# First attention of a megakernel: spikes added in PSUM, 128 tokens ahead of the rest, two powers on ScalarE, three currents on VectorE

## The reference

```python
# L0, first half: spiking mixer on h = layernorm(x)*(1+ca)+sa
r, ek, v = sigmoid(h@Wr+br), exp(h@Wk+bk), h@Wv+bv
# scan over time: wkv from running sums, inp = r*wkv
mem = 0.3*mem + inp - (mem > 0.05)*0.05
x = x + ga * (mem > 0.05)            # the spikes
# L0, second half: two layers (l = 0, 1) of local attention and MLP on
h = layernorm(x)*(1+cb) + sb
h2 = shift_token(h)                  # upper 64 channels one token later
q, k, v = split(h2 @ wqkv[l])        # 8 heads of 64
q, k = rotary(l2norm(q)*qs), rotary(l2norm(k)*ksc)
h = h + local_attention(q, k, v, window=64) @ wo[l]
h = h + gated_mlp(layernorm(shift_token(h)))
x = x + gb * h
# L1: linear recurrence, then experts (8, the best two) on x
```

## Time and profile before

| | us |
|---|---|
| median of 3 timed runs | 548.56 (548.49 to 548.58) |
| profiled execution, device time | 549.87 |
| its span | 548.1 |
| TensorE busy | 494.0 (90%) |
| VectorE busy | 427.0 (78%) |
| ScalarE busy | 349.6 (64%) |
| GpSimd busy | 339.3 (62%) |

### The profile page before, as it was taken

The page is one execution under the profiler, slowest core; times in us unless marked ns, Lnnn a source line. Parts: engine busy times, 40 slices in busy tenths (PEclk is TensorE's granted clock), DMA queues, the critical chain, the costliest instruction groups (busy, mean ns, idle before and its releaser), DMA issues.

```text
span 548.1 us, 11812 instructions
## 1 busy us (share of the span) xinstructions
PE 494.0 (90%) x4059; PEld 315.8 (58%) x4059; DVE 427.0 (78%) x1173; ACT 349.6 (64%) x1001; POOL 339.3 (62%) x271
## 2 busy tenths in 40 slices
PE   5844088999999999999899999999999999999996
PEld 5424033567777776443467777777544445667775
DVE  6999999899888976566889988995545687566665
ACT  5854007699999987534679999998556526533332
POOL 5990028999999998668989999994111277410000
PEclk9975579999999999999989999999999999999999
DMA  8600003211111112000221111111000000000000
GB/s 300 238 1 1 0 3 109 56 39 32 40 40 41 41 39 71 0 2 0 77 49 35 37 41 39 41 40 31 1 1 0 0 1 1 1 1 19 22 20 19
DMA packets 15025, 20.98 MB, mean 38 GB/s; under 512 B 2379, under 2 KB 9013, under 8 KB 14709
## 3 DMA queue, kind: packets, MB, share of 16 engines
q1 hardware_dynamic: 14676, 20.13, 13.3%
q10 hardware_dynamic: 288, 0.08, 0.1%
HBM read 9.99 MB, written 1.05 MB: 20 GB/s over the span
## 4 chain that ended last, share of the span: by engine, by line
PE 68%; DVE 18%; POOL 6%; issue 4%; ACT 3%; DMA 1%; DVEq 0%; SPq 0%; POOLq 0%; ACTq 0%
PE psT L1523 11%; PE psQK L1615 9%; PE psO L1738 6%; PE psO L1670 5%; PE psQK L1945 5%; PE psS L1718 5%; DVE vst L1108 3%; DVE vAB L1112 3%; PE psO L1523 3%; PE psS L2017 3%; PE psQK L1752 3%; PE psO L2017 2%; PE psQK L1877 2%; PE psS L1854 2%; PE psQK L1756 2%
## 5 line engine op out<-in xcount | busy, mean ns | idle before, releaser
L576 ACT ACTIVATE prob<-psS,nmx 128x128 f32<-128x128 f32 x256 | 90.1, 378 | 18.2 <-DVE nmx L1248 18.2
L904 POOL TENSOR_TENSOR rn<-ssq,half 128x16 f32<-128x16 f32 x32 | 93.2, 2913 | 8.6 <-DVE ssq L1234 8.5
L896 POOL TENSOR_TENSOR ra<-ra,rb 128x512 f32<-128x512 f32 x64 | 81.0, 1286 | 1.0 <-DVE rb L1216 0.8
L716 POOL TENSOR_TENSOR rst<-mv,half 128x4 f32<-128x4 f32 x24 | 25.7, 1072 | 73.8 <-DVE mv L1009 64.2
L1615 PE MATMUL psQK<-wqkv,hsA 128*128 128x512 f32 x128 | 62.0, 604 | 1.0 <-DVE hsA L1197 0.6
L576 ACT ACTIVATION_READ_ACCUMULATOR prob<-psS,nmx 128x1 f32 x256 | 55.4, 216 | 0.0
L912 POOL TENSOR_TENSOR qkn<-ra,rn 128x512 f32<-128x512 f32 x32 | 49.0, 1532 | 2.5
L1213 DVE TENSOR_TENSOR ra<-psQK,rope 128x512 f32<-128x512 f32 x64 | 43.9, 686 | 7.5 <-PE psQK L1615 6.6
L1216 DVE TENSOR_TENSOR rb<-psQK,rope 128x512 f32<-128x512 f32 x64 | 43.5, 680 | 0.0
L697 ACT ACTIVATE gel<-psQK 128x512 f32<-128x512 f32 x32 | 19.1, 597 | 37.5 <-PE psQK L1945 37.5
L1227 DVE TENSOR_REDUCE ssq<-sq 128x8 f32<-128x512 f32 x64 | 41.1, 676 | 1.6 <-ACT sq L516 1.3
(11 more groups left out here) (263 smaller groups left out, 1177.6 us busy)
## 6 DMA issues: line engine op xcount, KB each, us to landing
vAB<-vAB SPq DMA_DIRECT2D x62, 128.0 KB, 2.2
wqkv<-in_wqkv SPq DMA_DIRECT2D x2, 768.0 KB, 8.2
big<-in_x SPq DMA_DIRECT2D x4, 256.0 KB, 5.3
ra<-in_rope_t SPq DMA_DIRECT2D x1, 1024.0 KB, 7.7
ropeb<-in_rope SPq DMA_DIRECT2D x1, 1024.0 KB, 8.6
big<-in_ew SPq DMA_DIRECT2D x2, 512.0 KB, 4.1
wmod<-in_wmod SPq DMA_DIRECT2D x2, 384.0 KB, 6.8
out<-big SPq DMA_DIRECT2D x3, 256.0 KB, 2.3
```

The costliest lines, as they stand in the source:

```text
L576: act.activation(prob[:, k, :], psS[:, hb, c * P:(c + 1) * P], ACT.Exp, bias=nmx[:, k:k + 1], accum_out=sums[:, n % 2, k:k + 1]).then_inc( ...
L896: pool.tensor_tensor(o, o, rb[:, r], ALU.add).then_inc(s["sum_" + name], 1)
L904: pool.tensor_tensor(rn[:, :], ssq[:, :], half[:, :], ALU.pow).then_inc(s["rn_ready"], 1)
```

## The change

Seven things, all around the first tiles of layer 0:

1. VectorE takes current 1 too, from the PSUM bank, before quotient 3; GpSimd keeps current 2 only.
2. The thresholds write to a row of their own, `spikes` (big[:, 6, :]). x_cm is transposed into the four statistics banks while the membrane passes run, and TensorE then adds the spikes to each bank with ordinary products by the identity (`stack_t1`, start=False). All four thresholds come before the first statistics. x_cm itself gets the spikes at the end of layer 0, all groups on GpSimd.
3. The expert weights, whose place `spikes` has taken, are loaded in layer 1, after that layer's weights.
4. `first_norm`: ScalarE takes the first power as exp(-0.5 ln x), GpSimd only multiplies. ScalarE normalises two blocks, scales the first 128 tokens from a bank of their own into z, and then does the rest.
5. VectorE copies only these 128 tokens to hsA; the remaining 384 of group 0 go by two transfers, which the products of tiles 1 to 3 wait for.
6. `norms(0)`, the power for tile 0, is ScalarE's too, ahead of the fourth group's normalisation. The activation table that holds both functions is loaded in the place of the old load.
7. The order on all engines follows: statistics of groups 2 and 3 between tile 0's rotary products on VectorE, tile 1's products between the later transposes on TensorE.

The core of the diff:

```diff
+                    sp.wait_ge(s["ln_out"], ln_no(1, 0) + 1)
+                    sp.dma_start(hsA[0:64, P:GW], z[0:64, P:GW]).then_inc(s["hsA_dma0"], 16)
+                    sp.dma_start(hsA[64:128, P + 1:GW + 1], z[64:128, P:GW]).then_inc(s["hsA_dma0"], 16)
+                else:
                     sp.wait_ge(s["x_mixed"], NG)
...
                 act.wait_ge(s["num_ready"], min(g + 2, NG))
-                act.activation(rsg[:, gsl(g)] if g in (1, 2) else r_bank(g), r_bank(g), ACT.Sigmoid, bias=vec[:, V_BR:V_BR + 1]).then_inc(s["r_ready"], 1)
+                act.activation(rsg[:, gsl(g)] if g == 2 else r_bank(g), r_bank(g), ACT.Sigmoid, bias=vec[:, V_BR:V_BR + 1]).then_inc(s["r_ready"], 1)
...
             act.wait_ge(s["table"], 1)
+            act.preload_act_table_set("natural_log_exp_and_others")
             load_table(ACT.Exp)
...
-            ln_norm(ln_no(1, 0))
-            stack_out(0)
+            def power(dst, src):
+
+                own.one(act.activation(dst, src, ACT.Ln, bias=0.0, scale=1.0))
+                return act.activation(dst, dst, ACT.Exp, bias=0.0, scale=-0.5)
+
+            def first_norm():
+
+                n = ln_no(1, 0)
+                act.wait_ge(s["ln_var"], n + 1)
+                power(rst[:, n % 4, :], mv[:, n % 4, :, 1]).then_inc(s["rst_act"], 1)
+                act.wait_ge(s["rst_act"], 1)
+                act.wait_ge(s["ln_rstd"], n + 1)
+                act.wait_ge(s["ln_t2"], n - 1)
+                for k in range(TPG):
+                    act.activation(lnx[:, n % 2, k, :], stat_bank(n)[:, k, :], ACT.Identity, bias=nmr[:, n % 4, k:k + 1],
+                                   scale=rst[:, n % 4, k:k + 1]).then_inc(s["ln_norm"], 1)
+                    if k == 1:
+                        act.wait_ge(s["first_t2"], 1)
+                        act.activation(z[:, 0:P], psQK[:, 0, 0:P], ACT.Identity, bias=mod[:, 0, SB, 0:1],
+                                       scale=mod[:, 0, CB, 0:1]).then_inc(s["first_out"], 1)
+                act.wait_ge(s["ln_t2"], n + 1)
+                act.activation(z[:, P:GW], out_bank(n)[:, P:GW], ACT.Identity, bias=mod[:, 0, SB, 0:1],
+                               scale=mod[:, 0, CB, 0:1]).then_inc(s["ln_out"], 1)
+
+            def norms(n):
+
+                act.wait_ge(s["ssq_max"], n + 1)
+                if n:
+                    act.wait_ge(s["k_ready"], n)
+                    act.wait_ge(s["q_ready"], n)
+                power(rn[:, :], ssq[:, :]).then_inc(s["rn_ready"], 1)
+
+            first_norm()
             ln_norm(ln_no(1, 1))
+            squares_k(0)
             ln_norm(ln_no(1, 2))
             stack_out(1)
-            squares_k(0)
             squares_q(0)
+            norms(0)
             ln_norm(ln_no(1, 3))
...
                 elif n == 0:
-                    act.wait_ge(s["x_mixed"], NG)
+                    act.wait_ge(s["spikes"], 2)
                 act.activation(vB[:, u, :], psO[:, 1, :], ACT.Copy).then_inc(s["v_evac"], 1)
...
             rough(3)
-            current(1)
             current(2)
...
             pool.wait_ge(s["r_ready"], NG)
-            pool.wait_ge(s["cur_ready"], 2)
+            pool.wait_ge(s["cur_ready"], 1)
             for k, edge in enumerate((hsA[64:128, T:T + 1], hsA[64:128, 0:1], hsM[64:128, T:T + 1], hsM[64:128, 0:1])):
...
                 pool.wait_ge(s["edges"], k + 1)
-            def add_spikes(g):
-
-                pool.wait_ge(s["x_mixed"], g)
-                if g == 3:
-                    pool.wait_ge(s["spk"], 1)
-                pool.tensor_tensor(x_cm[:, gsl(g)], x_cm[:, gsl(g)], ekv[:, gsl(g)], ALU.add).then_inc(s["x_mixed"], 1)
-
-            add_spikes(2)
-            ln_rstd(ln_no(1, 0))
-            add_spikes(3)
-            for g in range(1, NG):
-                ln_rstd(ln_no(1, g))
+            n = ln_no(1, 0)
+            pool.wait_ge(s["rst_act"], 1)
+            pool.tensor_tensor(nmr[:, n % 4, :], nmean[:, n % 4, :], rst[:, n % 4, :], ALU.mult).then_inc(s["ln_rstd"], 1)
+            ln_rstd(ln_no(1, 1))
+            ln_rstd(ln_no(1, 2))
...
                 if has(i + 2):
-                    norms(n + 2)
+                    if n + 2:
+                        norms(n + 2)
                     k_normed(n + 2)
...
                     rope_sum(n + 3, 1)
+                    if n + 3 == 0:
+                        ln_rstd(ln_no(1, 3))
                     rope_sum(n + 3, 0)
...
                 if l == 0:
+                    pool.wait_ge(s["spikes"], 2)
+                    for g in range(NG):
+                        pool.tensor_tensor(x_cm[:, gsl(g)], x_cm[:, gsl(g)], spikes[:, gsl(g)], ALU.add).then_inc(s["x_mixed"], 1)
                     phase_scalars()
...
             current(0)
+            current(1)
             quotient(3)
             current(3)
-            dve.wait_ge(s["cur_vec"], 2)
+            dve.wait_ge(s["cur_vec"], 3)
...
-                steps.did(dve.tensor_scalar(by_chunk(ekv, g), of_group(ph, g, 1), -1.0, mod[:, 0, GA, bof(g):bof(g) + 1],
+                steps.did(dve.tensor_scalar(by_chunk(spikes, g), of_group(ph, g, 1), -1.0, mod[:, 0, GA, bof(g):bof(g) + 1],
                                             ALU.is_lt, ALU.mult))
+            dve.wait_ge(s["xT_evac"], NG)
             threshold(own, 0)
...
-            def add_spikes(g):
-
-                dve.wait_ge(s["xT_evac"], g + 1)
-                dve.tensor_tensor(x_cm[:, gsl(g)], x_cm[:, gsl(g)], ekv[:, gsl(g)], ALU.add).then_inc(s["x_mixed"], 1)
-
             own.sync()
-            add_spikes(0)
-            add_spikes(1)
+            dve.memset(cend[:, 0, 0:1], 0.0).then_inc(s["spikes"], 1)
+            dve.tensor_scalar(by_chunk(spikes, NG - 1), of_group(ph, NG - 1, 1), -1.0, mod[:, 0, GA, B - 1:B],
+                              ALU.is_lt, ALU.mult).then_inc(s["spikes"], 1)
             ln(ln_no(1, 0))
-            threshold(Steps(dve, s["spk"]), 3)
             ln(ln_no(1, 1))
-            ln(ln_no(1, 2))
...
-            dve.wait_ge(s["ln_out"], ln_no(1, 0) + 1)
-            shifted(hsA, z, 0, "hsA_ready")
+            dve.wait_ge(s["first_out"], 1)
+            dve.tensor_copy(hsA[0:64, 0:P], z[0:64, 0:P]).then_inc(s["hsA_first"], 1)
+            dve.tensor_copy(hsA[64:128, 1:P + 1], z[64:128, 0:P]).then_inc(s["hsA_first"], 1)
+            ln(ln_no(1, 2))
+            dve.wait_ge(s["rope_ready"], 4)
+            rope_products(0, 1)
             ln(ln_no(1, 3))
-            dve.wait_ge(s["rope_ready"], 4)
-            qk_first(0)
+            rope_products(0, 0)
+            sum_squares(0, 1)
+            sum_squares(0, 0)
+            clamped(0)
             rope_products(1, 1)
+            q_normed(0)
             rope_products(1, 0)
-            q_normed(0)
...
                     b = bof(g)
+                    dve.wait_ge(s["x_mixed"], NG + g)
                     dve.scalar_tensor_tensor(out=x_cm[:, gsl(g)], in0=z[:, gsl(g)], scalar=mod[:, 0, GB, b:b + 1],
...
                 g = i // TPG
-                if l == 0 and g or g == NG - 1:
+                if l == 0 and i == 0:
+                    pe.wait_ge(s["hsA_first"], 2)
+                elif l == 0 or g == NG - 1:
                     pe.wait_ge(s[f"hsA_dma{g}"], 32 * (l + 1))
                 else:
-                    pe.wait_ge(s["hsA_ready"], 2 * (l + g + 1))
+                    pe.wait_ge(s["hsA_ready"], 2 * (g + 1))
...
             pe.wait_ge(s["xT_evac"], NG)
-            pe.wait_ge(s["r_ready"], NG)
+            pe.wait_ge(s["rope_ready"], 4)
+            pe.wait_ge(s["mod_raw"], 1)
+            for g in range(NG):
+                for k in range(TPG):
+                    mm(stat_flat(ln_no(1, g))[:, k * P:(k + 1) * P], x_cm[:, g * GW + k * P:g * GW + (k + 1) * P], ident[:, :],
+                       is_transpose=True, start=(k == 0), stop=(k == TPG - 1), skip_group_check=True)
             pe.wait_ge(s["ld_wa"], 64)
...
             pe.wait_ge(s["init"], 3)
-            pe.wait_ge(s["mod_raw"], 1)
             pe.wait_ge(s["cnt_ready"], 1)
...
             keep_clock(10, psO[:, 0, :])
-            pe.wait_ge(s["rope_ready"], 4)
             def stack_t1(g):
-                pe.wait_ge(s["x_mixed"], g + 1)
-                four(stat_flat(ln_no(1, g)), lambda k: x_cm[:, g * GW + k * P:g * GW + (k + 1) * P]).then_inc(s["ln_t1"], 1)
+                pe.wait_ge(s["spikes"], 1 + (g == NG - 1))
+                for k in range(TPG):
+                    i = mm(stat_flat(ln_no(1, g))[:, k * P:(k + 1) * P], spikes[:, g * GW + k * P:g * GW + (k + 1) * P], ident[:, :],
+                           start=False, stop=(k == TPG - 1), skip_group_check=True)
+                i.then_inc(s["ln_t1"], 1)
...
             stack_t1(2)
-            keep_clock(10, psT1[:, :])
-            ln_t2(ln_no(1, 0))
             stack_t1(3)
+            keep_clock(2, psT1[:, :])
+            first = ln_no(1, 0)
+            pe.wait_ge(s["ln_norm"], TPG * first + 1)
```

(10 more changed lines are left out.)

## The result

The changed kernel takes 552.55 us (median of four runs, 551.94 to 553.49) against 548.52 us of the kernel before: ratio 1.0075, 95% interval 1.0059 to 1.0091. It is 4.0 us slower where I forecast 1.95 us faster. The profiled execution took 553.49 us, with a span of 551.7.

A forecast was written before the change was run, and what follows sets the result against it. Bound: TensorE's steady attention loop from about 111 us, entered late through GpSimd's rounds. Tile 2's power comes -1.35 - 0.7 = -2.0 earlier, 1.95 carried, other terms 0: 548.56 - 1.95 = 546.6 us, range 546.0 to 547.2.

The forecast's parts named there:

- Currents: Before the membrane, moving current 1 to VectorE leaves the last current ending at 38.5: term 0, bounds -0.25 and +0.3.
- Spikes in PSUM: Before the first statistics, TensorE adds the spikes, first group ready at 78.4 as now: term 0.
- First power: Way into the attention: two ScalarE activations and a multiply replace GpSimd's power, normalising starts at 80.75, -1.05.
- 128 tokens ahead: First group: first key product at 82.4 instead of 85.90 (-3.5), second at 87.5 instead of 89.34 (-1.8).
- Power of tile 0 and what is late next: First attention: clamp at 89.65, norm 4.1 earlier, k out only 1.35 earlier, plus 0.7 at tile 2's clamp: -2.0.
- rival at 549.8: Powers on ScalarE force table loads, two activations and at least 2.6 us: 549.8, chance 0.02.
- the two rivals with a slow clock: Way in: clock falls between 84.5 and 87.5, 547.6, chance 0.10; spike products run at 1.2 GHz, 550.1, chance 0.03.
- End of layer 0: GpSimd's four additions, 5.0 us, make the power 1.0 late against 2.3 of room: term 0, bounds 0 and +1.2.
- the 3.70 stays: End of layer 0: upper bound +1.2, if GpSimd's 3.70 us operation keeps its length when moved off VectorE's copies.
- Expert loads: Start of layer 1: at 386 GB/s the queue drains 2.8 later, at 278, values used at 279.8: term 0, cover 1.7.
- The clock: Rival: the clock fall at 273 to 274 behind TensorE's 1.9 us pause goes too, -1.5 to 545.1, chance 0.12.

The follow-up runs named there:

- mended_cur_pool: mended with current 1 back on GpSimd, so VectorE makes two of the four currents and GpSimd two; 547.38 us, ratio 0.9977 to the kernel before.
- before_loads: The kernel before with only the two expert loads issued in layer 1 behind its other weight loads; 550.50 us, ratio 1.0040.
- mended: The changed kernel with GpSimd's four spike additions at the end of layer 1 and the expert loads behind all layer 1 value transfers; 547.50 us, ratio 0.9981.
- split: The changed kernel with GpSimd's 3.65 us add-and-add operation written as two of multiply and add; 551.12 us, ratio 1.0042 to the kernel before.

## Why the prediction was wrong

- **Currents, term 0**: right (mended_cur_pool). **Spikes in PSUM, term 0**: right, statistics at 78.26 (forecast 78.4).
- **First power, -1.05**: the start at 80.75 is as forecast. As the power's own worth it was too high: undoing it costs 0.56, because the same power on GpSimd then takes 1.02 and not 1.42.
- **128 tokens ahead**: right, 82.74 and 87.69 against 82.4 and 87.5.
- **Power of tile 0 and what is late next**: the clamp was at 90.12 and not at 89.65. The walk had ScalarE's row in the right order, but too short: from its first output, which ended at 84.87 and not at 84.5, it was 0.26 late at the end of the query's squares, and VectorE's last reduction (0.69 from 89.33) and the gap ahead of the clamp took 0.2 more. These 0.47 us went on to k, which was out at 96.49: -0.86 instead of -1.35. The vanished stretch of the clamp was right in kind (0.17 instead of 0.69), but it is 0.52 and not 0.7. Sum -1.40 instead of -1.95: mechanism right, one term 0.5 too large. No table load stands among the new powers (rival at 549.8; 546.6 and its 2.6 make 549.2), and the granted clock is full from 76 to 94 us, so the two rivals with a slow clock there fell too.
- **End of layer 0, term 0**: the step that failed first. The 3.70 us were read as VectorE's doing, though the operation takes 3.64 us wherever it runs, at 236.08 in the kernel before too. The rest of the reckoning was right: GpSimd was to be 1.0 us late against its neighbours with an operation of 1.12, and 2.5 us more make the 3.5 that were measured. Against 2.3 us of room that loses 1.2, which is the upper bound that I had written down and not taken ("the 3.70 stays"); TensorE waited 1.37. A second charge stood nowhere in the sum: I never asked what GpSimd's later 128x1024 operations would lie beside, and one fell on a copy, 1.1 us. Together 2.47 (from -1.40 at 110.54 to +1.07 at 274.33).
- **Expert loads, term 0, cover 1.7**: the second failure. I took 386 GB/s from the fastest microsecond that the trace of before showed; the three behind it had 361, 231 (it is in the earlier trace rows) and 238. In the changed kernel the nine windows from 272 to 281 us have 254 on average. Counted from the start of the eight transposes, the queue was empty after 2.2 us in the kernel before (275.5), after 6.8 in before_loads (279.9) and after 7.7 in the changed kernel (282.0): 4.6 and 5.5 us later, where I had 2.8. The cover was too large as well. The value product starts 6.5 us behind the transposes in the profile before (279.77), but 5.0 in mended (276.76), where the clock stays up; so 1.5 of the 1.7 us of cover were the fall of the clock. In before_loads and in the changed kernel the product starts as the queue falls empty, at 279.84 and 282.01. Alone the loads cost 2.2 us by the ratio of before_loads.
- **The clock**: I tied its fall to a pause and to the program's phase. It fell at 273 in the profile before, at 283 in that after, and at neither place in mended, whose pause of 1.88 us at the same place is unchanged, nor in split, which has the pause of 2.56 us as well. What decides it is open. The fall at 273 costs 0.95 us by the table above, not 1.5.

In the two profiles the places add up. From +1.07 at the eight transposes it goes to +3.77 at the later pair of products, which is the loads' 1.95 (as in split), plus 1.7 for the fall of the clock behind the pause, less the 0.95 that the kernel before paid at 273; the spans differ by 3.6. The medians differ by 4.0, and -1.4 + 2.5 + 2.2 (before_loads) is 3.3. How often the timed runs have these falls isn't known, so what makes the last 0.7 us of the medians is not shown.

## What to carry to other kernels

A step moved off the critical stretch must be priced in the order of its new place: what runs beside it, what stands behind it on its engine, and what those will now lie beside. Before a long row is put down to its neighbours, look for the same operation where it has none; here the trace of before had it twice more, at the same length. Idle time of GpSimd is no free place if VectorE copies there. Loads without a deadline go behind every transfer that has one.

## What the runs showed of the hardware that I had not expected

- GpSimd's tensor_scalar of add and add on 128x1024 takes 3.64 to 3.70 us, that of multiply and add 1.04 to 1.16: in split two of the second take 2.18 us from start to end, 1.5 us less than one of the first.
- A VectorE instruction on 128x4 elements takes 1.18 us instead of 0.17 beside a GpSimd addition of 128x512, while GpSimd's additions nearly keep their length (two in 2.54 us there; three in 3.73 in mended, where nobody copies). The kernel before has such a place as well: a step of the second group's statistics takes 1.17 us from 81.85, beside GpSimd's addition of spikes from 81.74 to 83.00.
- The same pause of TensorE at 272 us, 1.88 us long, is followed by the lower clock level in two profiles (before, mended_cur_pool) and by the upper in others (mended, split, before_loads), and a pause of 2.56 to 2.57 us at 280 by the lower in one (after) and the upper in another (split).
